# Splitting each pair of score tiles around the step's piece in four attention loops

## The reference

```
x = x + L0_attn(layernorm(x))   # window and global mask, distance slopes, rotary, 8 key heads
x = x + L0_ffn(layernorm(x))    # SwiGLU
x = x + L1_attn(layernorm(x))   # causal
x = x + L1_ffn(layernorm(x))    # table of splines
x = x + L2_attn(layernorm(x))   # causal, rotary
x = x + L2_ffn(layernorm(x))    # experts of 128 to 512
x = x + L3_attn(layernorm(x))   # no mask; heads and batch scrambled in the output
x = x + L3_ffn(layernorm(x))    # experts, two of eight

scores = einsum(q, k) / sqrt(16);  p = softmax(scores);  a = einsum(p, v);  out = a @ Wo
```

## Time and profile before

| | |
|---|---|
| median of three runs | 1841.24 us (1839.78 to 1844.73) |
| the profiled execution | 1843.98 us, its span 1842.2 us |
| TensorE matmul busy | 1603.0 us, 87% of the span |
| VectorE busy | 1163.0 us, 63% |
| ScalarE busy | 867.6 us, 47% |
| GpSimd busy | 468.5 us, 25% |
| mean granted TensorE clock | 0.937 |

### The profile page before, as it was taken

How to read it: one execution, slowest core, us unless ns; L and a number is a source line. 1 busy time by engine, 2 the same in 40 slices (tenths; PEclk the granted TensorE clock), 3 DMA queues, 4 the chain that set the end, 5 groups by cost and what they waited for, 6 DMA issues and landing times. The chain is left out here.

```text
span 1842.2 us, 27440 instructions
## 1 busy us (share of the span) xinstructions
PE 1603.0 (87%) x9702; PEld 922.0 (50%) x9702; DVE 1163.0 (63%) x3079; ACT 867.6 (47%) x1361; POOL 468.5 (25%) x596
## 2 busy tenths in 40 slices
PE   4899999799989999843999999689999999997776
PEld 2344444388855555442445555467764444443543
DVE  2687787433447666577678776455536688774475
ACT  1255565523325554541245555357751666664322
POOL 4222210023332330011333220046763421300000
PEclk9899899999989999975999999779999999989698
DMA  7451350200235424001552450302206335411222
GB/s 247 102 133 59 86 137 7 92 0 0 67 100 161 127 75 121 1 9 40 160 142 78 121 144 1 108 23 64 92 1 186 115 81 126 124 37 32 92 92 92
DMA packets 68957, 160.07 MB, mean 87 GB/s; under 512 B 10285, under 2 KB 15926, under 8 KB 67962
## 3 DMA queue, kind: packets, MB, share of 16 engines
q1 hardware_dynamic: 68826, 158.38, 30.2%
HBM read 108.92 MB, written 53.09 MB: 88 GB/s over the span
## 5 line engine op out<-in xcount | busy, mean ns | idle before, releaser
L1366 ACT ACTIVATE a_pT<-PS 128x1024 f32<-128x1024 f32 (+3 forms) x384 | 310.2, 811 | 238.9 <-PE PS L1449 166.1
L1167 DVE CUSTOM_DVE_ANT_0 PS<-PS,cst 128x384 f32<-128x384 f32 (+3 forms) x512 | 244.6, 511 | 107.8 <-PE PS L1424 96.9
L1424 PE MATMUL PS<-a_k,a_q 64*128 64x512 f32 (+3 forms) x768 | 240.5, 422 | 29.0 <-DVE a_mx L1167 20.2
L1170 DVE TENSOR_REDUCE a_mx<-PS 128x1 f32<-128x512 f32 x256 | 164.4, 685 | 58.7 <-PE PS L1424 58.0
L440 DVE CUSTOM_DVE_ANT_0 PS<-PS,a_dist 128x448 f32<-128x448 f32 x256 | 156.1, 643 | 56.6 <-PE PS L685 54.3
L1440 PE MATMUL PS<-a_q,a_k 64*128 64x512 f32 (+3 forms) x768 | 174.1, 441 | 10.0 <-issue 6.4
L1463 PE MATMUL PS<-a_pT,a_va 128*32 128x512 f32 (+3 forms) x1536 | 168.5, 511 | 3.1 <-ACT a_raw L1319 2.9
L590 ACT ACTIVATE a_pT<-PS 128x448 f32<-128x448 f32 (+1 forms) x256 | 124.6, 540 | 87.9 <-PE PS L708 87.5
L1424 PEld LDWEIGHTS PS<-a_k,a_q 64*128 64x128 f32 x768 | 110.7, 190 | 100.6 <-DVE a_mx L1167 45.9
L1440 PEld LDWEIGHTS PS<-a_q,a_k 64*128 64x128 f32 x768 | 75.8, 188 | 152.1 <-issue 75.6
L157 PE MATMUL PS<-cst 128*128 128x512 f32 x192 | 101.2, 657 | 36.7 <-PEq L98 28.6
(11 more groups left out here) (360 smaller groups left out, 3350.7 us busy)
## 6 DMA issues: line engine op xcount, KB each, us to landing
spread_scratch<-a_high SPq DMA_DIRECT2D x96, 256.0 KB, 3.8
a_q<-spread_scratch SPq DMA_DIRECT2D x96, 256.0 KB, 5.6
a_k<-spread_scratch SPq DMA_DIRECT2D x96, 256.0 KB, 6.4
f_gb<-gate_rows SPq DMA_DIRECT2D x68, 256.0 KB, 5.3
spread_scratch<-a_low SPq DMA_DIRECT2D x48, 256.0 KB, 3.7
a_q<-window_scratch SPq DMA_DIRECT2D x32, 256.0 KB, 5.5
a_k<-window_scratch SPq DMA_DIRECT2D x32, 256.0 KB, 6.4
window_scratch<-a_high SPq DMA_DIRECT2D x24, 256.0 KB, 4.6
```

Source lines behind the costliest of these rows:

```text
L1167: dve.tensor_tensor_reduce(tile, tile, cst[:, C_LATER + S - kw:C_LATER + S], 1.0, -3e38, ALU.add, ALU.max, dst).then_inc(max_done, 1)
L1170: dve.tensor_reduce(dst, tile, AX.X, ALU.max).then_inc(max_done, 1)
L1366: act.activation(pT[:, N // 2 % 2, N % 2, :, q0:S], PS[:, 2 * (N % 2):2 * (N % 2) + 2, q0:S], ACT.Exp, scale=SCALE).then_inc(exp_done, 1)
L1424: pe.matmul(ps[:, 0:kw], q[b % 2][rows, pair, qt * P:(qt + 1) * P], k[b % 2][rows, pair, 0:kw], start=True, stop=True).then_inc(s_done, 1)
```

## The change

In the loop of both attention functions the second score tile of a step moves behind the step's piece on TensorE, and its maximum moves behind the piece on VectorE. On VectorE the piece itself also moves behind the exchange and the layer-norm work of the step. The masks within the maxima are as before; nothing is added or removed, and GpSimd's, ScalarE's and the DMA queues' programs stay as they were. The prologues stay too.

```diff
@@ attention_window, VectorE
                 for N in range(FULL):
-                    for t in (2 * N + LEAD, 2 * N + LEAD + 1):
-                        if t < NB * TILES_:
-                            minima(t)
-                    piece(*piece_at(N))
+                    if 2 * N + LEAD < NB * TILES_:
+                        minima(2 * N + LEAD)
                     if N % STEPS in swaps and N // STEPS + 1 < NB:
                         exchange(N // STEPS + 1, swaps[N % STEPS])
...
                         elif N % STEPS == 28:
                             sigmoid(c)
+                    piece(*piece_at(N))
+                    if 2 * N + LEAD + 1 < NB * TILES_:
+                        minima(2 * N + LEAD + 1)
@@ attention_quads, VectorE
                 for N in range(FULL):
-                    for t in (2 * N + LEAD, 2 * N + LEAD + 1):
-                        if t < NB * TILES_:
-                            maxima(t)
-                    piece(*piece_at(N))
+                    if 2 * N + LEAD < NB * TILES_:
+                        maxima(2 * N + LEAD)
...
                         layer_norm_apply(dve, ln, N // STEPS + 2, source(N // STEPS + 2))
+                    piece(*piece_at(N))
+                    if 2 * N + LEAD + 1 < NB * TILES_:
+                        maxima(2 * N + LEAD + 1)
@@ attention_quads, TensorE (attention_window the same)
                 for N in range(FULL):
                     scores_T(N)
-                    for t in (2 * N + LEAD, 2 * N + LEAD + 1):
-                        if t < NB * TILES_:
-                            scores(t)
+                    if 2 * N + LEAD < NB * TILES_:
+                        scores(2 * N + LEAD)
                     if N % 2 and N >= 3:
                         values((N - 3) // 2)
                     piece(*piece_at(N), previous_piece(N))
+                    if 2 * N + LEAD + 1 < NB * TILES_:
+                        scores(2 * N + LEAD + 1)
```

## The result

| | before | changed |
|---|---|---|
| median | 1841.24 us | 1822.18 us (1818.71 to 1828.7, 5 runs) |
| profiled execution, span | 1843.98, 1842.2 us | 1818.7, 1816.9 us |
| loops a0 / a1 / a2 / a3 | 269.0 / 237.8 / 237.7 / 255.7 us | 258.1 / 238.5 / 240.5 / 242.7 us |

The ratio is 0.9894, 95% interval 0.9861 to 0.9927. The kernel is 19 us faster, where 46 were forecast: 41% of the gain. The new time lies just above the likeliest case's own range (1766 to 1821) and inside the wider one (to 1830). The profiled execution is the fastest of the five, so its loops show the gain rather too large.

A forecast was written before the change was run, and what follows sets the result against it. TensorE and VectorE wait for each other in turn, so the order of work bounds the kernel. Gains of 20 + 13 + 4 + 10 = 47 us off 1844.0 give 1797, stated as a 1795 us median; range 1766 to 1821, 8-in-10 to 1830.

The forecast's parts named there:

- likeliest case: Whole kernel: a gain of 20 to 75 us, 1795 us with range 1766 to 1821, chance 0.70.
- part one: TensorE, second score tile behind values and piece: 0.20 us gained per wait, 20 us in a3, 13 in a1.
- The walk: Five steps of a3 timed on paper: ends at 9.27 instead of 10.31 us, 1.04 us for four holds.
- rival A: VectorE's order, including the copy of the maxima, eats the gain: 1830 us, chance 0.10.
- Part two: VectorE, piece and exchange ahead of the second maximum: gain of 10 us in a0, 4 us in a2.
- Part three: TensorE row halves: lone second tile shares its slot with the next transposed scores, costed at nothing.
- rival B: Split tile pair doesn't share its slots: up to 1954 us; chance 0.06 including a weaker slow case.
- GpSimd: Its split waits for the last of 16 maxima, later now: costed at nothing, 30 us if cover is gone.
- D: Nothing moves, the waits only change their place: 1841 us, chance 0.06.
- C: Nearly all holds vanish and VectorE follows: gain of 90 us, 1751 us, chance 0.08.

The follow-up runs named there:

- e17: The changed kernel run a second time, nothing altered: 1825.31 us, ratio 0.9922.
- e10: Changed kernel with VectorE's copy of the maxima behind the second maximum in a1 and a2 only: 1810.02 us, ratio 0.983.
- e11: e10 with long and short score tiles exchanged in the causal loops: 1858.48 us, ratio 1.0102.
- e14: Changed kernel with the old order restored in the causal loops a1 and a2, the new order kept in a0 and a3: 1820.02 us, ratio 0.9894.
- e15: Changed kernel plus nine unused 128x512 matmuls in the last sequence of each causal loop: 1825.38 us, ratio 0.9932.
- e16: e10 plus nine unused 128x512 matmuls in the last sequence of each causal loop: 1811.36 us, ratio 0.9841.

## Why the prediction was wrong

**The step that failed is part one, the gain of 0.20 us for each wait, and most of all its carrying over to a1**: "I use the same 0.20 us: 64 x 0.20 = 13 us". Part one forecast 33 us in a3 and a1; they gave 12.3. The walk behind the 0.20 promised 1.04 us for four holds, and the same five steps gained 0.54, at full clock before and after: 0.135 us each. In a1 two things came on top, and the sum had neither.

- *The clock.* The causal loops spent 65.8 us at the lower level (1.2 GHz) instead of 37.5. At 0.30 to 0.39 us each that is an estimate of 8 to 11 us of the some 21 that a1 and a2 fall short. In a0 and a3 it went the other way (23.9 us at the lower level before, 6.8 after), so over the four loops the clock takes only an estimate of 3 to 4 of the 27 us that are missing. The rest is the gain per wait that was sized too large. Sequences with no low clock in either profile show the order alone: a1's third took 61.6 us before and 59.8 in e17, a gain of 1.8 us and not 13 / 4 = 3.25. In a3 the first three took 196.7 and 189.2 us, 2.5 each and not 20 / 4 = 5.
- *The copy.* The forecast had it as rival A, but said that a walk which has the copy in it still gains. In a1 the steps around the copy do not (6.08 to 6.11 us): 1.23 us stand ahead of a maximum of 0.30 us. Of the 10.9 us that e10 gains in a1 against the changed kernel, the 18.0 us less of lower clock are an estimate of 7, and sixteen steps by 0.24 us the other 4. The gain at those sixteen steps is shown; how much of the clock follows from it is not, since with one and the same order a1 had 27.3 us of lower clock in one profile and 6.8 in another.

**Part one in a3 had its mechanism right and its size wrong**: 13.0 us instead of 20, and of these 13.0 an estimate of 3 to 4 are the 10.2 us of lower clock that the last sequence had before and no longer has. The walked stretch ended at 9.27 on paper; the same five steps took 1514.46 - 1504.69 = 9.77 against 10.31 before. Two terms were too small. From a lone tile's load to its maximum I used 0.43 us, the idle time; load to start was already 0.66 in the trace of before (1520.07 to the earlier trace rows's 1520.73), and after the change it is 0.54. TensorE's load of before, then VectorE's row for the tile loaded at 1504.68 after the change:

```profile
1520.07 0.47 PEld L1424 LDWEIGHTS PS<-a_k,a_q 64*128 64x128 f32 x2
```

```profile
1505.22 1.29 DVE L1172 TENSOR_REDUCE a_mx<-PS 128x1 f32<-128x512 f32 x2 [0.36 <-PE PS L1427]
```

And from a first tile to the piece or the values behind it I used 0.33; it is 0.42 (1504.97 to 1505.39, 1506.56 to 1506.98), and the earlier trace rows had 0.43 already (1516.80 to 1517.23, 1518.53 to 1518.96). The walk has five such places, 0.45 us if none of them is hidden, against the 0.50 that it fell short.

**Part two** was right in a0 by number (10.9 for 10), of which an estimate of 2 to 3 us are 6.9 us less of lower clock. It was off in a2 (+2.8 for -4); 5.1 of these 6.8 us lie in the last sequence, at the lower clock. The mechanism named for a2, about 0.3 us more idle time before each rotation, did not appear. VectorE in a2 waited for the projection ahead of its rotations (us in all, times, longest), before:

```profile
DVE a_comp L1194 <- PE PS L1401: 12.1, 12, 2.3
```

and in the changed kernel:

```profile
DVE a_comp L1196 <- PE PS L1404: 10.3, 12, 2.1
```

**Part three** was right, and with it rival B is out. The lone second tile and the next transposed scores load at 1504.68 and 1504.69, and both at 1505.98, as the earlier trace rows had it, and their matmuls start at the same times. The Trainium skill, page "TensorE: Matmul & The Clock Gate", section "The mechanism", says that matmuls on distinct row groups overlap; by that rule, the trace agrees for these 64-row tiles. Its other half, that they end in program order, would cost an estimate of 5 us in the causal loops; no run tested it.

**GpSimd** at nothing: no row points to it. In all four loops TensorE's waits put down to the split came to 1.6 us before and 1.3 after, both in a2. It was not tried by itself.

**The rivals.** A (1830) was the nearest in number and names part of the cause, the copy; D (1841) is out by the interval; C's gain never appears, not even in e10. I gave the forecast 0.70 on the strength of one walk in the one loop without mask or rotation. What stays open is what sets the clock: the same work in a slightly different order spends 24 us of a1 at the lower level in e10 and 61 in e11. The windows show what goes with it: length less matmul time of a1 is 11.1 us before, 11.5 in e10, but 19.8 in the changed kernel and 21.9 in e11. Whether the idle time brings the lower level is not shown; e14 had 11.8 us of it with only 6.8 at the lower level, where before had 27.3.

## What to carry to other kernels

When a walk gives a gain per wait, walk one stretch in each kind of loop before multiplying, and try every long instruction (here a copy of 1.23 us) behind the short one that another engine waits for, loop by loop: the copy gained in a1 and a2 and lost in a0 and a3, and the exchange lost in a0. Count the end-to-end time from one engine's start to the other's, and not the idle time that the trace lists. Afterwards compare loop lengths and granted clock, sequence by sequence, since sums of waits doubled here while the kernel got faster. Sequences that ran at full clock in both profiles tell the worth of an order closely (a3's third took 63.3 to 63.4 us in all ten profiles with the changed order there); whole loops do not.

## What the runs showed of the hardware

The time at the lower clock level differed widely over kernels with the same work: in a1 from 6.8 us (e14) to 61.4 (e11). The order has a part in it, since the changed order had more of it than that of before in two profiles each, but one order alone gave 6.8 and 27.3. Each such us cost 0.30 to 0.39 us of a loop in which two engines wait for each other, and about 0.5 on a step full of matmuls. With nine unused matmuls added to a last sequence, the lower level there went from 17.1 and 13.7 us to 0.0 and 3.4 (e15), and from 10.2 and 13.7 to nothing (e16); the kernels got no faster.
